# Spreading the row maxima on VectorE, and four 512-column matmuls instead of sixteen of 128 in an attention stage

## The reference

```python
xn = layernorm(x, ln1_w, ln1_b)
yn = layernorm(y, ln2_w, ln2_b)
q = (xn @ Wq).reshape(B, N1, H, hd).transpose(0, 2, 1, 3)
kv = (yn @ Wkv).reshape(B, y.shape[1], 2, H, hd)
attn = jax.nn.softmax(jnp.einsum('bhqd,bhkd->bhqk', q, k) * scale, axis=-1)
o = jnp.einsum('bhqk,bhkd->bhqd', attn, v).transpose(0, 2, 1, 3).reshape(B, N1, C1)
x = x + (o @ Wproj + bproj)
h = jax.nn.gelu(layernorm(x, ln3_w, ln3_b) @ W1 + b1, approximate=False)
x = x + (h @ W2 + b2)
```

## Time and profile before

| | |
|---|---|
| median of 3 runs | 370.87 us (367.78 to 372.27) |
| profiled execution, its time | 367.57 us |
| its span | 365.7 us |
| TensorE matmul busy | 348.2 us, 95% of the span |
| VectorE busy | 266.0 us, 73% |
| ScalarE busy | 230.1 us, 63% |
| GpSimd busy | 198.7 us, 54% |

### The profile page before, as it was taken

The page is one execution under the profiler, slowest core; times in us unless marked ns, Lnnn a source line. Parts: engine busy times, 40 slices in busy tenths (PEclk is TensorE's granted clock), DMA queues, the critical chain, the costliest instruction groups (busy, mean ns, idle before and its releaser), DMA issues.

```text
span 365.7 us, 10716 instructions
## 1 busy us (share of the span) xinstructions
PE 348.2 (95%) x4315; PEld 311.9 (85%) x4315; DVE 266.0 (73%) x583; ACT 230.1 (63%) x424; POOL 198.7 (54%) x179
## 2 busy tenths in 40 slices
PE   8989999999999898899999999999999999999985
PEld 6978888888888776689999999999998888877664
DVE  5899988899899975349776585655798559676433
ACT  2457677767666664671745637457469768886771
POOL 2664644565666540116766856657399828655300
PEclk9999999999999999999999999999999999999999
DMA  6864001020000010000000000000000000000001
GB/s 157 238 198 129 28 27 30 24 55 26 3 3 2 3 45 2 2 2 23 22 24 0 23 2 22 23 3 2 2 0 2 2 16 31 30 17 30 31 31 57
DMA packets 13928, 12.50 MB, mean 34 GB/s; under 512 B 2996, under 2 KB 13240, under 8 KB 13880
## 3 DMA queue, kind: packets, MB, share of 16 engines
q1 hardware_dynamic: 13872, 11.83, 11.4%
q10 hardware_dynamic: 8, 0.00, 0.0%
HBM read 9.73 MB, written 2.10 MB: 32 GB/s over the span
## 4 chain that ended last, share of the span: by engine, by line
PE 73%; DVE 13%; issue 5%; ACT 4%; DMA 2%; SPq 1%; POOL 1%; DVEq 0%; ACTq 0%; POOLq 0%
PE banks_s L1140 12%; PE bank_o L930 6%; PE banks_s L978 5%; PE bank_y L1149 5%; PE bank_t L1149 5%; PE banks_s L1244 5%; DVE row_max L1782 3%; PE bank_y L1061 3%; PE bank_t L1033 3%; PE bank_qk L955 2%; PE bank_o L969 2%; PE bank_t L930 2%; PE bank_qk L959 2%; DMA bproj_row<-in_L_xattn_bproj 2%; DVE max_cols L1788 2%
## 5 line engine op out<-in xcount | busy, mean ns | idle before, releaser
L451 POOL TENSOR_TENSOR norm_q_inv<-norm_q_min,minus_half 128x32 f32<-128x32 f32 x8 | 43.8, 5475 | 19.4 <-DVE norm_q_min L1953 17.9
L439 POOL TENSOR_TENSOR norm_k_inv<-norm_k_min,minus_half 128x32 f32<-128x32 f32 x8 | 44.1, 5516 | 8.7 <-DVE norm_k_min L1921 8.7
L350 POOL TENSOR_TENSOR masked<-qkT_r,halves_t 128x512 fp32r<-128x512 f32 x32 | 32.8, 1046 | 21.2 <-DVE qkT_r L1772 21.2
L562 ACT ACTIVATE PT<-banks_s 128x1024 f32<-128x1024 f32 x32 | 31.0, 1022 | 20.3 <-PE banks_s L1015 18.3
L1782 DVE TENSOR_REDUCE row_max<-banks_s 128x8 f32<-128x1024 f32 x32 | 37.7, 1218 | 7.5 <-PE banks_s L978 7.4
L730 ACT ACTIVATE PT<-banks_s 128x1024 f32<-128x1024 f32 x32 | 31.0, 1024 | 5.7 <-PE banks_s L1244 5.7
L1140 PE MATMUL banks_s<-lnT_hi,W_hi 128*128 128x256 f32 x120 | 34.2, 285 | 0.0
L1140 PE MATMUL banks_s<-lnT_hi,W_lo 128*128 128x256 f32 x120 | 33.9, 282 | 0.0
L1140 PE MATMUL banks_s<-lnT_lo,W_hi 128*128 128x256 f32 x120 | 33.9, 282 | 0.0
L1734 DVE TENSOR_TENSOR hT_lo<-W_s,hT_hi 128x512 fp32r<-128x512 f32 x32 | 21.9, 690 | 16.3 <-ACT hT_hi L667 16.2
L978 PEld LDWEIGHTS banks_s<-masked,qkT_r 32*128 32x128 f32 x768 | 25.0, 183 | 9.5 <-issue 7.7
(11 more groups left out here) (285 smaller groups left out, 1052.9 us busy)
## 6 DMA issues: line engine op xcount, KB each, us to landing
x_all<-in_x SPq DMA_DIRECT2D x16, 128.0 KB, 2.1
W_s<-in_L_xattn_W SPq DMA_DIRECT2D x2, 1024.0 KB, 7.6
out<-x_all SPq DMA_DIRECT2D x16, 128.0 KB, 1.7
ctx_in<-in_ctx SPq DMA_DIRECT2D x16, 96.0 KB, 2.3
ctx_in<-in_ctx_T SPq DMA_DIRECT2D x8, 128.0 KB, 2.3
ctx_in<-in_ctx_T SPq DMA_DIRECT2D x8, 64.0 KB, 2.5
Wq_s<-in_L_xattn_Wq SPq DMA_DIRECT2D x1, 256.0 KB, 3.5
Wkv_s<-in_L_xattn_Wkv SPq DMA_DIRECT2D x1, 256.0 KB, 3.5
```

Of the source, the lines that this page charges most:

```text
L350: nc.gpsimd.tensor_tensor(masked[:, r, 1, :, half, :], qkT_r[:, r, 1, :, :].bitcast(fp32), ones, ALU.mult)\
L439: nc.gpsimd.tensor_tensor(norm_k_inv[:, :], norm_k_min[:, :], minus_half[:, :], ALU.pow).then_inc(c_kinv, 1)
L451: nc.gpsimd.tensor_tensor(norm_q_inv[:, :], norm_q_min[:, :], minus_half[:, :], ALU.pow).then_inc(c_qinv, 1)
L562: nc.scalar.activation(PT[:, 2 * h:2 * h + 2, :], banks_s[:, 2 * h:2 * h + 2, :], ACT.Exp, scale=HD ** -0.5)\
```

## The change

`maxT` and `picks_wide` go. A new buffer `max_rows` (128x512) takes the negated maxima already spread over the heads' columns: one VectorE operation multiplies the turned maxima in PSUM, read once for each of the four heads, with `picks_t`, broadcast over 128 columns, so that rows of other heads become 0. `ones_r` (128x128 of 1.0) becomes the weights, and `shifted_a` issues four matmuls of 512 columns, one for each quarter. `maxima_T` moves from ScalarE's program to VectorE's, with its two waits: to the end of a step, behind `maxima` of the following tile; for the last two tiles ahead of and behind the last `maxima`.

```diff
-            maxT = sb_a("maxT", 128, TOK, dtype=fp32r)
-            picks_wide = sb_a("picks_wide", 128, GH, TOK, dtype=fp32r)
+            max_rows = sb_a("max_rows", 128, GH, TOK, dtype=fp32r)
+            ones_r = sb_a("ones_r", 128, TOK, dtype=fp32r)
...
-            def maxima_T(t, bank=bank_qk):
-
-                if ok(t):
-                    act.wait_ge(a_max_turned, t + 1)
-                    wait(act, a_shifted, t)
-                    nc.scalar.activation(maxT[:, :], bank[:, 0:TOK], ACT.Copy).then_inc(a_maxT, 1)
...
-            nc.scalar.activation(picks_wide[:, :, :], each(picks_t[:, :], GH, TOK), ACT.Copy).then_inc(picks_ready, 1)
+            nc.scalar.activation(ones_r[:, :], minus_half[:, 0:1].broadcast_to([128, TOK]), ACT.Copy, scale=-2.0).then_inc(picks_ready, 1)
...
-                    for r in range(GH):
-                        for g in range(QUARTERS):
-                            last = mm(bank_s[g][:, TOK * r:TOK * (r + 1)], picks_wide[quad(g), r, :], maxT[quad(g), :],
-                                      start=False, stop=r == GH - 1)
+                    for g in range(QUARTERS):
+                        last = mm(bank_s[g][:, :], ones_r[quad(g), :], max_rows[quad(g), :, :], start=False, stop=True)
...
+            def maxima_T(t, bank=bank_qk):
+
+                if ok(t):
+                    dve.wait_ge(a_max_turned, t + 1)
+                    wait(dve, a_shifted, t)
+                    v.tensor_tensor(max_rows[:, :, :], bank[:, 0:TOK].unsqueeze(1).broadcast_to([128, GH, TOK]),
+                                    each(picks_t[:, :], GH, TOK), ALU.mult).then_inc(a_maxT, 1)
...
                 queries_keys_lo(s - 1)
                 maxima(s - 2)
+                maxima_T(s - 3)
...
             maxima(1)
+            maxima_T(0, bank_y)
...
             maxima(2)
+            maxima_T(1)
             w1_split(0)
             w1_split(1)
...
             stats_b(1)
+            maxima_T(NB - 2, bank_t)
             maxima(NB - 1)
+            maxima_T(NB - 1, bank_t)
             residual_a(NB - 4)
```

More of the change, by code:

```diff
@@ L597, in step_a @@
                 values_a(s - 2)
-                maxima_T(s - 3)
                 inputs_T(s)
@@ L616, in _ @@
             queries_keys_hi(2)
-            maxima_T(0, bank_y)
             inputs_T(3)
@@ L624, in _ @@
             values_a(2)
-            maxima_T(1)
             inputs_T(4)
@@ L631, in _ @@
             exps_a(NB - 3)
-            maxima_T(NB - 2, bank_t)
             on_T(NB - 4)
@@ L636, in _ @@
             exps_a(NB - 2)
-            maxima_T(NB - 1, bank_t)
             raw_b(0)
```

## The result

| | before | after |
|---|---|---|
| median of 4 runs each | 369.48 us (367.78 to 372.27) | 375.70 us (374.19 to 378.18) |
| ratio, 95% interval | | 1.0154 (1.0090 to 1.0219) |
| profiled execution, its time | 367.57 us | 376.94 us |
| its span | 365.7 us | 375.2 us |
| busy: TensorE, VectorE, ScalarE | 348.2, 266.0, 230.1 us | 352.6, 275.9, 225.8 us |

The changed kernel is 1.5% slower.

A forecast was written before the change was run, and what follows sets the result against it. TensorE bounds the first attention stage, VectorE from step 12. Terms of +0.30, +5.17 and +0.1 make +5.6 us: 373.2 from the profiled 367.57, named 376.5 because that lies 3.3 below the median; range 370.0 to 380.5.

The forecast's parts named there:

- slower by over 2%: Rival: the new VectorE operation costs more than L1772; at 0.76 us of queue the loss reaches 7.4 us; chance 0.26.
- steps 5 to 7: First attention stage, each from tile s-2's row maxima to the next tile's; TensorE-bound, each giving back 0.16 us.
- The matmuls save nothing: Rival: each matmul waits for weights loaded after the wait; +7.0 us, 377.9; no separate chance, inside the forecast's 0.48.
- The circle: Waits from VectorE's maxima through the new operation and TensorE's matmuls and scores to the next maxima: 7.96 us plus c.
- steps 9, 11, 13 and 15: Attention steps where TensorE would wait for the new operation: +0.33, +0.33, +0.99 and +1.02 us.
- only the queue counts: Rival: the circle doesn't close and the cast's delay stays; VectorE's queue alone costs +3.2 us, 374.1 by the median; chance 0.20.
- the cast's delay: Called c: extra time of VectorE's small cast L1788 while GpSimd runs its queue; 0.04 to 1.59 us by step.
- step 15's wait: TensorE's wait for the residual at 131.40 us, said to take up 0.7 of its lateness, leaving +1.02.
- The sum: All terms added: +0.30 by step 8's maxima, +5.17 for steps 8 to 15, +0.1 net in the tail; +5.6 us.
- steps 10, 12 and 14: Attention steps whose length VectorE sets, through 0.60 us more queue and the cast's delay: +0.61, +1.17 and +0.32 us.
- What would show it wrong: Signs: VectorE idle in steps 12 to 14, new operation above 0.85 us, or c off by more than 0.3 us.
- The start: Before step 5, VectorE's operations for tiles 0 and 1 add 0.18 and 0.60 us: +0.78, no cover left.

The follow-up runs named there:

- the first two experiments: Two runs: four wide matmuls with ScalarE spreading the maxima by four copies, against before, 0.9953; the changed kernel with sixteen 128-column matmuls again, 380.16 us, 1.0242.
- the first experiment: Kernel before with four 512-column matmuls, ScalarE spreading the maxima in four scaled copies, VectorE's program unchanged: median 367.87 us, ratio 0.9953.

## Why the prediction was right, and where not

The forecast was 376.5 us, +1.5%, and 375.7 with 1.0154 was measured. The mechanism holds; that the total is so close is partly luck, for two errors of opposite sign lie in it, and both medians lie in the gap between the two groups of starts (between 368.09 and 370.87, and between 374.46 and 376.94).

*The operation.* 0.69 us forecast, 0.68 measured, 0.60 of the queue. It isn't held by GpSimd: at 137.94 it takes 0.68 while GpSimd's addition L383 (137.22, 1.39 us) runs, as long as in the other steps, in which GpSimd's queue has ended or is about to end when it starts. With that the rival "slower by over 2%", which had 0.26 by the price of this operation, falls. The Trainium skill (SBUF — State Buffer, Who interferes with whom) has that a VectorE instruction with at most one SBUF input, outside the 2-port modes, doesn't contend with GpSimd, and the trace agrees in that one step.

*The matmuls.* 0.33 us forecast and measured, the saving 0.16 us in steps 5 to 7 (-0.48 as forecast). "The matmuls save nothing" falls with the first two experiments. (Step 5 of the kernel before is 8.29 us, not 8.32 or 8.33 as the prediction has it of steps 5 to 11.)

*The circle.* TensorE waits for L1784 in steps 9, 11, 13 and 15 as forecast (8.66, 8.66, 9.55 and 10.10 us forecast; 8.71, 8.70, 9.60 and 10.13 measured). It also does in steps 12 and 14, by 0.55 us at the weight loads, which the prediction didn't name. With the splits moved it doesn't wait in steps 8 to 14, and 0.42 us in step 15. But its worth was misread. As a difference to the rival "only the queue counts" (+3.2 us in all) it looked like 2.4 us; the run without it shows 0.63 in these steps. That rival was mis-sized because it left the cast's delay as it was and let step 15's wait hide the rest: without the circle step 12 is 1.44 us longer than before (9.78 for 8.34; the cast grows from 0.55 to 1.40) where the rival had 0.60, and step 15 is 0.58 longer (9.66 for 9.08) where it had nothing. The sum itself had the exchange of wait and hold in it (step 14's c 0.95 for 1.23, where the run without the circle keeps the cast at 1.40), the rival had not.

*The cast's delay c.* Forecast 0.95 in steps 12 and 14, measured 0.94 - 0.17 and 0.93 - 0.17, that is 0.77 and 0.76; forecast 0.24 in step 10, measured 0.07. These three terms make steps 10, 12 and 14 0.22, 0.19 and 0.20 us too long in the sum, which gave +5.17 for steps 8 to 15 where +4.64 was measured (the other five steps are together 0.08 too short in it). c was too large because VectorE's wait ahead of those maxima was taken too short: 0.3 us for step 12, where step 11 leaves VectorE 8.70 - 8.21 = 0.49 us idle, 0.39 of it just ahead of the maxima at 104.33. In step 13 it is right: 1.73 - 0.17 = 1.56 for 1.59.

*What would show it wrong.* VectorE has 0.51 us idle in step 13 (9.09 of 9.60), which the prediction named as a sign against it. That sign was badly chosen: in a step whose length the circle sets, VectorE must idle.

*The start.* +0.78 forecast, and right. Ahead of the maxima of tile 1 only a set-up activation is changed. From there to step 5 the traces of the kernel before, with its splits in place and moved, take 15.77 us each, and the five traces of the changed kernel and its variants with a full clock there 16.51 to 16.53: +0.75. The first tile's step is set-up: 5.53 us in the trace of before, 5.28 in that of before with the splits moved and in that after. So the +1.98 of the trace after is 0.75, less 0.25 of set-up, and 1.48 of low clock.

*The step that was missing.* No term of the sum had TensorE's clock, since the trace of before shows 1.00 throughout. The forecast counted TensorE's wait in step 15 as 1.02 us of length, and not that a wait could lower the clock behind it. In all ten executions of the changed kernel the mean granted clock is 0.993 to 0.995, in those of before 0.996 to 1.000. With the waits filled the loss is 372.7 to 373.0 against 367.5 to 368.5 us and 376.5 against some 371.8, about 4.8 us; without, 374.6 and 378.6, about 6.5. The stretches say the same: 0.75 - 0.48 + 4.64 - 0.07 = 4.84 us without a fall, and 1.48 to 1.66 for one. The sum's 5.6 lies between: 0.8 too much in its own terms, some 1.6 missing.

*The base.* The forecast was put on the median of before, 370.87 us, which is a run of the long start. By the start its 376.5 is to be held against the long starts of the changed kernel, 376.9 to 378.8 us, and the sum from the profiled time, 373.2, against its short ones, 374.2 to 374.6: both are too low.

## What to carry to other kernels

An operation moved to an engine with 27% idle time over the span still costs its whole length where that engine is the bound of the stage, and more where it pushes a small operation under another engine's hold: count the steps in which the engine has no idle time, and look at what its late operations will meet. Where two delays feed each other (here a wait and a hold), take one away in thought and see whether the other grows, before pricing them separately. A new wait on TensorE may have a price of its own behind it, in the clock. And compare executions of the same start: the median of the first experiment said 0.5% faster, and the runs of one start were the same within 0.1%.

## What the runs showed of the hardware that was not expected

TensorE's granted clock fell to about half (0.53 and 0.54 over 3.6 us) behind waits of only 1.3 to 1.7 us in a program that otherwise keeps it 94% busy, though not behind every such wait, and each fall cost 1.5 to 1.7 us; thirteen transposes of the identity in the wait of step 15 took the fall there away. The Trainium skill (TensorE: Matmul & The Clock Gate, HAM oscillation — how this bites in real kernels) tells of a clock that falls when TensorE waits for a DMA's data between bursts of matmuls; the traces agree in kind, with a wait for VectorE in the DMA's place, 1.69 to 1.70 us idle ahead of the falls in step 15.

A VectorE cast of 16 columns that takes 0.17 us alone took 1.73 to 1.79 us, until two GpSimd instructions in a row (L397 with 0.72 us and L410 with 1.27 us) had ended, without slipping in between them. Where a GpSimd cast stands behind L397 (step 9: L397 from 80.34, 0.73 us) it took 0.50 and ended with L397, and the subtraction behind it took 0.52.
